# Inverse roots in ten vector operations, and mean squares taken from the variance and the root, in a two-layer attention and expert kernel

## What is computed

```python
def _layernorm(x, axis=-1, eps=1e-05):
    m = jnp.mean(x, axis=axis, keepdims=True)
    v = jnp.var(x, axis=axis, keepdims=True)
    return (x - m) / jnp.sqrt(v + eps)

def rms_norm(x, scale):
    norm = jnp.mean(x * x, axis=-1, keepdims=True)
    return scale * (x * jax.lax.rsqrt(norm + EPS_RMS))
...
x = _layernorm(x + _L0_attn_ref(...), axis=-1)
x = _layernorm(x + _L0_ffn_ref(...), axis=-1)
x = _layernorm(x + _L1_attn_ref(...), axis=-1)
x = _layernorm(x + _L1_ffn_ref(...), axis=-1)
```

## Time and profile before

| what | value |
|---|---|
| median of three runs | 1810.16 us |
| the profiled execution, its own time | 1827.05 us |
| its span, first to last instruction | 1825.3 us |
| mean granted TensorE clock | 0.876 |
| PE busy | 1480.0 us, 81% |
| DVE busy | 957.6 us, 52% |
| ACT busy | 693.6 us, 38% |
| POOL busy | 498.8 us, 27% |

### The profile page before, as it was taken

One profiled execution on the slowest core, in us unless ns is written; L12 is line 12 of the kernel. 1 busy time (PEld: TensorE's weight loads), 2 busy tenths in 40 slices (PEclk: granted clock), 3 DMA queues, 4 the chain that ended last, 5 costly groups with the idle time before them and its releaser, 6 DMA issues.

```text
span 1825.3 us, 31302 instructions
## 1 busy us (share of the span) xinstructions
PE 1480.0 (81%) x10329; PEld 968.2 (53%) x10330; DVE 957.6 (52%) x3689; ACT 693.6 (38%) x957; POOL 498.8 (27%) x422
## 2 busy tenths in 40 slices
PE   3688888888978828999649999999998629999970
PEld 1244454444544525666425555555555429999970
DVE  3657766767667531111175767776843344444424
ACT  1143443433434511110017566666676402222222
POOL 4121323234132431121210122222121234444430
PEclk8788797787878868999869999999998759999995
DMA  6735346343350306352234446435626324444448
GB/s 160 190 89 96 81 94 136 77 97 83 88 107 15 105 15 199 94 136 73 46 70 93 94 96 134 111 77 111 130 61 177 131 65 70 70 72 72 70 72 254
DMA packets 122238, 182.88 MB, mean 100 GB/s; under 512 B 17111, under 2 KB 104561, under 8 KB 114432
## 3 DMA queue, kind: packets, MB, share of 16 engines
q1 hardware_dynamic: 98336, 151.84, 34.2%
q0 software_dynamic: 21504, 27.76, 9.2%
q10 hardware_dynamic: 2272, 1.67, 0.3%
HBM read 111.47 MB, written 77.02 MB: 103 GB/s over the span
## 4 chain that ended last, share of the span: by engine, by line
PE 56%; DVE 17%; issue 7%; DMA 5%; ACT 4%; POOL 1%; another core or an unknown queue 1%; SPq 1%; DVEq 0%; ACTq 0%; POOLq 0%
PE ST L1796 7%; PE shared L1808 7%; PE ST L702 6%; PE OT L720 6%; PE ST L1262 6%; DVE scratch L1094 4%; PE shared L746 3%; PE OT L1270 3%; PE shared L1270 3%; PE shared L794 2%; PE shared L1457 2%; DMA x_in<-sum 2%; PE shared L811 2%; PE shared L763 2%; PE shared L801 2%
## 5 line engine op out<-in xcount | busy, mean ns | idle before, releaser
L835 ACT ACTIVATE arena<-ST 128x1024 f32<-128x1024 f32 x416 | 414.6, 1025 | 333.3 <-PE ST L702 316.5
L1094 DVE CUSTOM_DVE_ANT_0 scratch<-shared,mask 128x512 bf16<-128x512 f32 (+3 forms) x512 | 229.1, 487 | 119.0 <-PE shared L811 102.1
L702 PE MATMUL ST<-arena 96*128 96x256 bf16 (+2 forms) x1792 | 258.3, 282 | 15.3 <-DMA arena<-qk_parts 13.2
L720 PE MATMUL OT<-arena,v_aug 128*32 128x256 f32 (+1 forms) x3584 | 261.5, 394 | 4.1 <-POOL arena L1162 2.7
L702 PEld LDWEIGHTS ST<-arena 96*128 96x128 bf16 (+1 forms) x1792 | 161.8, 104 | 119.8 <-issue 50.9
L811 PE MATMUL shared<-arena 96*128 96x512 bf16 (+3 forms) x512 | 133.0, 340 | 54.7 <-DVE mx L1094 26.4
L1162 POOL TENSOR_SCALAR_AFFINE_SELECT arena<-arena 128x512 f32<-128x512 f32 (+1 forms) x96 | 78.6, 818 | 306.8 <-ACT arena L835 306.8
L1905 POOL DMA_INDIRECT sum<-arena,block_to_row x72 | 111.3, 1546 | 169.2 <-ACT arena L1859 157.7
L720 PEld LDWEIGHTS OT<-arena,v_aug 128*32 128x32 f32 x3584 | 86.5, 112 | 120.8 <-issue 69.7
L1808 PE MATMUL shared<-arena 128*128 x576 | 136.1, 379 | 0.0
L811 PEld LDWEIGHTS shared<-arena 96*128 96x128 bf16 x512 | 45.6, 105 | 136.7 <-issue 60.9
(11 more groups left out here) (208 smaller groups left out, 2387.4 us busy)
## 6 DMA issues: line engine op xcount, KB each, us to landing
arena<-qk_parts SPq DMA_DIRECT2D x224, 128.0 KB, 7.1
qk_parts<-qk_src SPq DMA_DIRECT2D x64, 384.0 KB, 2.6
arena<-qk_parts SPq DMA_DIRECT2D x32, 384.0 KB, 4.5
block_rows<-slot_x SPq DMA_DIRECT2D x72, 130.0 KB
arena<-qk_parts SPq DMA_DIRECT2D x32, 256.0 KB, 5.3
sum<-x_out SPq DMA_DIRECT2D x16, 512.0 KB, 2.9
arena<-in_experts_inter SPq DMA_DIRECT2D x7, 1024.0 KB, 5.0
arena<-in_experts_out SPq DMA_DIRECT2D x7, 1024.0 KB, 9.4
```

Source lines behind the costliest of these rows:

```text
L702: mm = pe.matmul(ST[n % 2][:, i * 256 + at:i * 256 + at + nq], K[par][0:rows, h, kb * P:(kb + 1) * P], Q[par][0:rows, h, q0:q0 + nq], star ...
L720: mm = pe.matmul(OT[32 * i:32 * i + 32, q0:q0 + nq], v_aug[par][:, kb, g * GH + i, :], PT[n % RING][:, i, at:at + nq], start=(u == 0), sto ...
L835: act.activation(PT[n % RING][:, :, :], ST[n % 2][:, :].rearrange("p (h n) -> p h n", h=GH), func, scale=ATT_SCALE).then_inc(L["exp"], 1)
L1094: taken = dve.tensor_tensor_reduce(out=junk[n % 2][:, at:at + m], in0=bank[:, at:at + m], in1=mask[:, 0:m], scale=1.0, scalar=LOW, op0=ALU ...
```

## The change

`rsqrt` refines an estimate three times. A round had four operations and now has three: the factor -0.5 goes into the squaring, and the addition of 1.5 into the last product. The chain is ten operations in place of thirteen; it is used once in `finish_dve`, twice in `c_combine_dve` and twice in stage E. In `c_combine_dve` the second pass of statistics over `x` (four `bn_stats`, four `bn_aggr`, two small operations) is replaced by three small operations on the variance and the root that are there already: the mean square of a normalized row is its variance times the square of its root. The piece counts become 20 and 33, and with them the lists of A and C move.

```diff
-N_LN = 23
-N_COMBINE = 40
+N_LN = 20
+N_COMBINE = 33
...
-RSQRT_STEPS = 13
+RSQRT_STEPS = 10
...
     yield from chain(dve.tensor_scalar(out.bitcast(I32), x.bitcast(I32), -0.5, RSQRT_MAGIC, ALU.mult, ALU.add))
     for _ in range(3):
-        yield from chain(dve.tensor_tensor(tmp, out, out, ALU.mult))
+        yield from chain(dve.scalar_tensor_tensor(out=tmp, in0=out, scalar=-0.5, in1=out, op0=ALU.mult, op1=ALU.mult))
         yield from chain(dve.tensor_tensor(tmp, tmp, x, ALU.mult))
-        yield from chain(dve.tensor_scalar(tmp, tmp, -0.5, 1.5, ALU.mult, ALU.add))
-        yield from chain(dve.tensor_tensor(out, out, tmp, ALU.mult))
+        yield from chain(dve.scalar_tensor_tensor(out=out, in0=tmp, scalar=1.5, in1=out, op0=ALU.add, op1=ALU.mult))
...
-        COMB = NORM + TB + TB + TB + 2 + RSQRT_STEPS + 1 + TB + 1
+        COMB = NORM + TB + 3 + RSQRT_STEPS + 1 + TB + 1
...
             for t in range(TB):
                 chain.unwaited(dve.tensor_scalar(x[:, t, :], x[:, t, :], c_mv[:, t, 0:1], small[:, 7, t:t + 1],
                                                  ALU.subtract, ALU.mult))
-            yield from chain.pause()
-
-            for t in range(TB):
-                chain.unwaited(dve.bn_stats(c_stats[:, t, :], x[:, t, :]))
-            yield from chain.pause()
-            settle(dve)
-            for t in range(TB):
-                chain.unwaited(dve.bn_aggr(c_mv[:, t, :], c_stats[:, t, :]))
-            yield from chain.pause()
-            yield from chain(dve.tensor_tensor(small[:, 3, :], c_mv[:, :, 0], c_mv[:, :, 0], ALU.mult))
-            yield from chain(dve.scalar_tensor_tensor(out=small[:, 3, :], in0=c_mv[:, :, 1], scalar=RMS_EPS,
-                                                      in1=small[:, 3, :], op0=ALU.add, op1=ALU.add))
+                yield
+
+            yield from chain(dve.tensor_tensor(small[:, 3, :], c_mv[:, :, 1], small[:, 7, :], ALU.mult))
+            yield from chain(dve.tensor_tensor(small[:, 3, :], small[:, 3, :], small[:, 7, :], ALU.mult))
+            yield from chain(dve.tensor_scalar(small[:, 3, :], small[:, 3, :], RMS_EPS, None, ALU.add))
```

## The result

The changed kernel takes 1828.3 us (median of six executions, 1817.3 to 1833.3) beside 1810.2 us for the kernel before (1805.6 to 1813.2): the ratio is 1.0084, 95% interval 1.0052 to 1.0116. By the ratio it is slower by some 15 us (the two medians lie 18 us apart) where 9.7 us of gain were forecast.

The account below looks back on a forecast made before the run. PE was taken to bound C's body, DVE chains C's start and E, mutual waits A. The terms sum to 9.7 us, from 1810.2 to 1800.5 us, range 1793 to 1809.

Parts of the forecast that it names:

- (a): C's start: second statistics and five small steps fewer on the DVE chain PE waits for, -3.0 us.
- fourth rival: Fused small operations take longer, costing 1.8 us over the exposed roots; about 1803 us, no separate chance, inside the forecast's range.
- (b): Stage E: two roots, each three small DVE steps shorter, -1.3 us; only 0.6 if the last load were late.
- (c): Ninth slots of A and C: one shorter root each on the path to `x_out`, -1.2 us.
- (d): C's body slots: the combine ends 1 to 2 us sooner and PE's waits at `ps` for `r_before` go, -2.2 us.
- (e): C's second slot: part of the wait for `o_nat` at its end goes, -0.5 us, between 0 and -2.3.
- (f): A's body slots: `x_out` sooner, `rT0` ahead of `av6`, gain before `r_before`; 0.3 us in each of five slots, -1.5 us.
- third rival: A loses: longer stand at `rT0` keeps the clock at 1.2 GHz, 12 us in six slots; 1814 us, chance 0.12.
- Put at nothing: A's seventh slot, whose list moves too: the prediction took no gain there.

Follow-up runs that it names:

- clean trace of before: Kernel before, unchanged, profiled again in a later execution without the waits at POOL's scatters: span 1810.6 us, measured time 1809.7 us (ratio 1.0003).
- after_again: Kernel after, unchanged, timed again on another chip beside the kernel before: 1826.9 beside 1807.5 us, ratio 1.0091.
- a_list_only: Kernel before with N_LN 20 for 23 and nothing else: 1806.6 beside 1807.5 us, ratio 0.9983.
- before_again: Kernel before, unchanged, profiled and timed once more: 1839.8 us, ratio 1.0003.

## Why the prediction was wrong

By its own steps, with the sizes from the clean trace of before and the traces of after:

- **(a) C's start, -3.0.** Right: PE's wait is 24.86 - 21.68 = 3.2 us shorter, and the fused operations stand 0.20 us apart in the root (0.16 us each, as the forms that they replace). The fourth rival (fused operations are dearer) falls.
- **(b) E, -1.3.** The chain of each half is shorter as said, but the second half's load is now late by 0.68 us (`<-DMA arena<-sum`, at 1808.69). From the first `bn_aggr` of this stretch to the last operation of the second root it is 14.19 us in the clean trace of before and 13.69 now: of the 1.26 us, 0.5 are left, nearly the case that the text named (0.6).
- **(c) The ninth slots, -1.2.** Right: 7.16 and 7.17 us in the clean trace of before, 6.54 and 6.55 now, 1.2 us in both.
- **(d) C's body, -2.2. The step that failed.** It asked what stands ahead of `ps` and `r_before`, found one wait and took it away. Those waits did go, and in the clean trace of before they are 0.4 us in all and not 2.2. What it left out is that a step also waits for the buffer it writes to. The text knew that buffers of `shared` are handed out in the order of the list, three in turn, and that most steps of C move; it never asked whose buffer `lg` takes over when `rT0` and `rT1` fall behind `on1`. It also had `x_in` 1 us later (the load is now issued 35.2 us into the third body slot, before 33.6) and DVE's wait of 4.30 us for it in hand, and looked for its cost only at `ps`. In place of -2.2 stand +35.1 us: 16.5 of waits and 18.6 of work at the lower clock.
- **(e) C's second slot, -0.5.** Right: the wait at its end is 3.5 us before and 3.0 after.
- **(f) A's body, -1.5.** The size was not seen, and the mechanism failed too: -17.3 us. `x_out` comes 0.6 us sooner, but PE does not stand less in A's body slots, it stands more, 60.0 us in place of 55.4. At `rT0` it waits 7.7 us in place of 6.6, and the last to come is not `x_out` (done at 324.0 in the slot whose row is shown above) but DVE's `mx`, at 324.7: `rT0` takes over the buffer of `mx14`, which DVE now empties behind all of `x_out`, and in before ahead of its last two tiles. This is the blind spot of (d) again, at some 0.7 us a slot. At `ps`, where the text saw its gain, PE waits over twice as long (five slots, first the clean trace of before, then after):

```profile
PE shared L771 <- DVE r_before L978: 3.6, 5, 0.9
```

```profile
PE shared L770 <- DVE r_before L977: 7.7, 5, 1.8
```

The whole gain is busy time, 21.9 us less of it, at a mean clock of 0.92 in place of 0.85. I took the level of the earlier trace rows as given in every slot. In after, three of the five `rT0` run at the full clock (0.66 us; four in `after_again`), in the clean trace of before one. In `a_list_only` PE waits 2.0 to 2.2 us there, and all five take 1.11 us. What decides the level is not shown, and the wait just before `rT0` doesn't: in after the two slow ones come after 1.59 and 1.37 us, the three fast ones after 1.59. The third rival saw that A's clock could move by more than the counted operations, and had the wrong sign.
- **Put at nothing.** A's seventh and eighth slot together gained 2.7 us, and C's lost 2.0. What this comes from is open.

The sum of (a) to (c), (e) and (f) as measured is some 23 us of gain, and the kernels with all new operations and C's list mended gained 14 to 24 us. The loss in C took it all back and some 15 us more. That the miss is not larger is luck: had (f) been worth the 1.5 us forecast, the loss in C would have stood almost alone, at some 30 us slower.

On the clock, the rows show 1.52 us of work in 5 us at the full clock and then 7 us at 0.56. The Trainium skill, "TensorE: Matmul & The Clock Gate", section "A second HAM failure mode: psum-queue depth-cycling", describes a kernel in which PE pauses between groups as it cycles through PSUM buffers, and the clock swings between its levels. These traces agree in part: here too the pause comes from a PSUM buffer (`shared` lies there), the clock falls behind it, and half of the cost is the clock; but it is one stand of some 3.5 us in a slot and not many short ones.

That the profiled execution was 16.9 us above the median was taken over as a constant. This did no harm to the sum, but the prices were read from a trace with waits at the scatters that other executions don't have: in it `r_before` costs 2.2 us in C's body, in the clean one 0.4.

## What to carry to other kernels

When a change moves steps in a list from which buffers are handed out, write down for each moved step which earlier step had its buffer and which engine empties it, and treat "emptied by an engine that waits for a transfer in between" as a dependency like any other. A count that only sizes a list (here 40 to 33) can cost more than the operations it stands for: time the arithmetic with the old list before the list is re-spread. Where PE runs with many short waits and a mean clock between the levels, read the level in several slots of several traces, and price the stage at both: here A's body moved by 17 us where 1.5 were counted.

## What was not expected of the hardware

The same kernel differs by 30 us between chips: the kernel before took 1839.5 and 1829.7 us on two and 1807.5, 1808.2 and 1806.0 on three others. Each chip was used at one time only, so the chip and the hour can't be told apart. In the traces from the first two, in the first trace of before too, ACT, DVE or PE stands for up to 8.7 us with no releaser on record in nearly every stretch in which POOL issues its eight indirect DMAs; in those from the others, and in the first trace of after, there is no such wait of over 1.5 us. One of A's ends, in `before_again` (ACT), and the same place in after:

```profile
544.11 0.60 ACT L840 ACTIVATE oT_raw<-OT 128x512 f32<-128x512 f32 x1 [5.28 <-remote]
```

```profile
510.78 0.60 ACT L839 ACTIVATE oT_raw<-OT 128x512 f32<-128x512 f32 x1
```

The wait of the earlier trace rows is one of them. Most of them end 4 to 11.6 us after the first of the eight, which are issued over 9 to 10 us. The cause stays open: what on those chips delays an engine while POOL scatters isn't in the trace, and the kernel with plain DMAs never ran on one of them.
